# Image 0's fusion, tokens, mixtures and the weights' mixing moved under image 1's gathers

## The chip, the cores and the metric

The kernel runs on one core of a Trainium2 chip. The metric is the device time of one execution in microseconds (us); lower is better. The core has five engines with a queue each: TensorE (PE), VectorE (DVE), ScalarE (ACT), GpSimd (POOL) and SyncE (SP, which here only issues DMAs), and 16 DMA engines that they share.

## The reference

Two images of 128 channels and 64 x 64 pixels go through one layer, in float32:

```python
x = x + conv_ref(ln_c(x), ...)      # four deformable branches, pool branch, fusion
t = to_tokens(x)                    # (2, 4096, 128)
t = t + ffn_ref(ln_t(t), ...)       # spectral convolution + short mixtures
```

`conv_ref` has four deformable convolutions with 49, 1, 1 and 9 taps (60 in all) and 256 output channels each. For every tap and pixel an offset is computed, four neighbours are gathered, blended by bilinear weights and a mask, and contracted with that tap's 128 x 256 weights. Each branch is group-normalised and rectified, joined with a pooled branch, mixed by a 1 x 1 convolution to 128 channels (the fusion), group-normalised over the image and rectified again. `ffn_ref` normalises each token, convolves the sequence with 16 long filters (through a blocked Fourier transform), multiplies by matrices mixed from four sets with softmax weights, and adds a short three-step mixture (`M_u`).

## The kernel before

The program is a row of stages, each a block that all engines leave together.

`stage_normalise` prepares image 0: layer norm, a table of pixel rows in DRAM to gather from, and the first offsets. `stage_branches` is the long one. It works through 16 groups of 512 pixels (8 of image 0, then 8 of image 1) with 60 taps each, so 960 iterations n ("taps" below). Everything is written out by hand with semaphores; each engine runs its own `for n in range(...)` loop, in order:

- POOL: `gather(g, k, j)`, L509, four indirect DMAs of 128 rows for a tap, into one of RING = 6 buffers G. It waits until the tap six before has been blended (`blended`).
- ACT: `corner0` (L541), the first of the four corners times its weight into `ps_a`; `copy_out` (L549), transposed sum to `sT`.
- DVE: `blend` (L666 the other three corners times their weights, L670, L674, L677 the additions; L677 frees the buffer).
- PE: `turn` (L779, four transposes) and `contract` (L791, the tap's weights R times `sT`, accumulated in `ps_y`); and the offset convolution of the next groups (L761), spread over 52 of 56 taps.
- SP: loads and stores.

The offsets of later groups are computed beside this. The four pixel tiles of a group are handled two taps apart (`tile_at`: `rows` L618 to L633 and `weights` L639 to L646 on DVE, with L649 the end of a tile), at n = 100 + 56 i to 107 + 56 i. With k = n mod 60, at k = 54 DVE measures three branches' outputs (six L682), at k = 4 the last one. Image 1's layer norm runs in the same way under image 0's taps. R holds the weights of all 60 taps in SBUF for the whole stage.

Four stages follow for both images at once: `stage_fuse` (load y, rectify L1062, fuse L1024, copy L1042, statistics L1163; and beside it the weights' mixing: `mix` L1148 to L1153, rounding L1055, L1158, and the filters' transforms L1016, L1050, L1141), `stage_sum` (L1217, L1227), `stage_tokens` (16 chunks: L1345 to L1411, stores L1288 and L1294) and `stage_mixtures` (16 regions, L1460, L1449). Then `stage_spectral`, both images in one loop, and `stage_output`.

Of the kernel before, what the change touches and what calls it, by code (L numbers as in the profile page):

```python
# [3 lines left out]


B, C, H, W = 2, 128, 64, 64
HW = H * W
O = 256
# [27 lines left out]
NFC = 2 * (NBR + 1)  # L36
F32 = mybir.dt.float32
# [7 lines left out]
class Steps:  # L45
# [5 lines left out]
    def then(self, ins):  # L51
        self.n += 1
        ins.then_inc(self.sem, 1)
        self.eng.wait_ge(self.sem, self.base + self.n)

# [214 lines left out]

def stage_branches(nc, x, xn, tables, wom, R, ps_shared, base, P, rowt, regw, ident, eps6, om_dram, y_dram, ystats, xpart):

    ctx = ExitStack()
    with ctx:
        sb = lambda name, shape, dt=F32: ctx.enter_context(nc.sbuf_tensor(name, shape, dt))
        sem = lambda name: ctx.enter_context(nc.semaphore(name))
# [19 lines left out]
        yb = [sb(f"yb{h}", [128, 2, CH]) for h in range(3)]  # L296
        YB = (0, 1, 2, 1)
# [32 lines left out]
        r_loaded = pair("r_loaded")  # L330
        gathered = [sem(f"gathered{s}") for s in range(RING)]
# [25 lines left out]
        ln_step = sem("x1_step")  # L357

# [44 lines left out]
        def _(sp):  # L403
# [49 lines left out]

            sp.dma_start(R[:, 0:WIN_TAP, :], regw[:, 0:WIN_TAP, :]).then_inc(r_loaded[0], 16)
# [17 lines left out]
            for n in range(NT + 5):  # L472
# [25 lines left out]
                if c is not None:  # L498
                    store_xn(c)
            for h in range(3):  # L500
                sp.wait_ge(stored[h], 16 + 16 * YB.count(h) * NG)

# [25 lines left out]
        def _(act):  # L528
# [49 lines left out]

            for m in range(AHEAD):
                sigmoid(m)  # L580
            for n in range(NT + LAG + 1):
# [19 lines left out]
                if c is not None:  # L601
                    copy_x(c)

        @block.vector
        def _(dve):
# [102 lines left out]

            for m in range(AHEAD):
                rows(m)  # L710
                weights(m)
            spread(0)
            for n in range(NT + 5):
# [21 lines left out]
                if c is not None:  # L735
                    total_x(c)
            dve.wait_ge(measured, NBR * NG + 2)
# [3 lines left out]
        def _(pe):  # L741
# [40 lines left out]
            def contract(n):  # L782
# [4 lines left out]
                if k == t0:  # L787

                    pe.wait_ge(evacuated, g * NBR + br + 2)
                for half in range(2):  # L790
                    last = nc.tensor.matmul(ps_y[:, half, :], R[:, k, 128 * half:128 * half + 128],  # L791
# [11 lines left out]
            def turn_xn(c):  # L803
# [3 lines left out]
                last.then_inc(xn_turned, 1)  # L807

# [4 lines left out]
            for n in range(NT):  # L813
# [19 lines left out]
                if c is not None:  # L833
                    turn_xn(c)
            for n in range(NT - LAG, NT):
# [9 lines left out]
def group_affine(dve, act_sem, st, sq, var, sd, a, b, gm, gamma, beta, ready, nc):  # L845

    st.then(nc.vector.tensor_tensor(sq, gm[:, 0, :], gm[:, 0, :], ALU.mult))
    st.then(nc.vector.tensor_tensor(var, gm[:, 1, :], sq, ALU.subtract))
    st.then(nc.vector.tensor_scalar(var, var, 0.0, None, ALU.max))
    dve.sem_inc(ready, 1)  # L850
    dve.wait_ge(act_sem, 1)
    st.then(nc.vector.reciprocal(sd, sd))
    st.then(nc.vector.tensor_tensor(a, gamma, sd, ALU.mult))
    st.then(nc.vector.tensor_tensor(b, gm[:, 0, :], a, ALU.mult))
    st.then(nc.vector.tensor_tensor(b, beta, b, ALU.subtract))


def stage_fuse(nc, gate, y_dram, ystats, xpart, pool_w, fuse_w, gnp, gnf, blk16, blk8, eps5, fu, fa, fb,
               phi, dft_taps, m_phi, m_u, sigma, logw, gumbel, mus, mh, ml, hot, kern_dram):

    ctx = ExitStack()
    with ctx:
        sb = lambda name, shape, dt=F32: ctx.enter_context(nc.sbuf_tensor(name, shape, dt))
        sem = lambda name: ctx.enter_context(nc.semaphore(name))
        pw = sb("pw", [C, O])
        fw = sb("fw", [128, NFC, C])
        gp = sb("gp", [128, 2, B, NFC])
        gf = sb("gf", [C, 2, B])
        mv = sb("mv", [128, B, 2 * NBR, 2])
        me = sb("me", [128, 2, B * NFC])  # L870
        gm = sb("gm", [128, 2, B * NFC])
        sq = sb("sq", [128, B * NFC])
        var = sb("var", [128, B * NFC])
        sd = sb("sd", [128, B * NFC])
# [1004 lines left out]
```

## Time and profile before

| | us |
|---|---|
| median of 3 runs (6341.73 to 6343.83) | 6341.98 |
| the profiled execution | 6341.62 |
| its span, first to last instruction | 6339.8 |
| mean granted TensorE clock in it | 0.937 |

The profile is of one execution. The page has busy times by engine, the span in 40 slices, and the costliest groups of instructions; the trace behind it answers questions by line, by stretch of time, by wait and in order of time. All rows used are shown further down. In them "issue" as a releaser means that an engine waited for nothing that the profile shows, and "SPq" is SP's queue.

### The profile page before, as it was taken

Reading aid. Unit: us, or ns where it says so; the run is one execution under the profiler, and the core shown is the slowest. Engines: PE = TensorE matmul, PEld = TensorE weight load, DVE = VectorE, ACT = ScalarE, POOL = GpSimd, SP = SyncE. Lnnn points to the kernel's source line nnn. Section 1 sums busy time; section 2 is a strip of 40 time slices with the busy share of each in tenths; the row PEclk is TensorE's granted clock in tenths of the full one; section 3 lists DMA queues with packets and bytes.
Section 4 is the critical chain, followed back from the end, with each engine's and each line's share of the span. In section 5 each row is a group of like instructions: output and inputs, shape, how many; then the busy total and the mean of one; then the engine's idle time right before and its main releaser. Section 6 shows DMA issues by size and latency. Waiting matters only on the chain. (4 is left out here: it accounts for less than half of the span.)

```text
span 6339.8 us, 66182 instructions
## 1 busy us (share of the span) xinstructions
PE 5183.8 (82%) x16608; PEld 2621.9 (41%) x16608; DVE 4852.1 (77%) x6696; ACT 2639.3 (42%) x6416; POOL 3943.7 (62%) x4379
## 2 busy tenths in 40 slices
PE   6987878888887888888787878875666759999998
PEld 5333333333333333333233333322222337777777
DVE  5897888878887888878788887878777364666664
ACT  1343434333333434333333333433333633666663
POOL 4777777777777777777777777777777002222221
PEclk8999999999999999999999999998888979999999
DMA  7777777777777777777777777777777864555555
GB/s 242 219 239 222 238 227 229 227 220 230 216 226 218 224 223 222 220 226 217 227 215 233 210 232 209 230 209 230 216 215 219 308 220 135 149 146 151 152 149 178
DMA packets 565020, 1349.89 MB, mean 213 GB/s; under 512 B 95111, under 2 KB 244490, under 8 KB 563338
## 3 DMA queue, kind: packets, MB, share of 16 engines
q0 software_dynamic: 328480, 1045.08, 56.4%
q1 hardware_dynamic: 216922, 282.50, 13.9%
q10 hardware_dynamic: 19344, 19.20, 0.9%
q8 instruction: 106, 1.74, 0.1%
q14 instruction: 168, 1.38, 0.1%
HBM read 1240.28 MB, written 106.13 MB: 212 GB/s over the span
## 5 line engine op out<-in xcount | busy, mean ns | idle before, releaser
L509 POOL DMA_INDIRECT G<-table,om x3840 | 3660.3, 953 | 1199.0 <-issue 1160.3
L666 DVE TENSOR_TENSOR G<-G,ps_w 128x1536 f32<-128x1536 f32 x960 | 1681.5, 1752 | 491.5 <-DMA G<-table,om 475.2
L791 PE MATMUL ps_y<-sT,R 128*128 128x512 f32 x3840 | 2015.7, 652 | 25.7 <-ACT yb L557 25.7
L541 ACT ACTIVATE ps_a<-G,om 128x128 f32<-128x128 f32 x3840 | 1192.6, 357 | 1871.6 <-DMA G<-table,om 1196.7
L779 PE MATMUL ps_t<-ident,acc 128*128 128x128 f32 x3840 | 661.9, 298 | 948.3 <-DVE acc L677 928.8
L779 PEld LDWEIGHTS ps_t<-ident,acc 128*128 128x128 f32 x3840 | 433.3, 147 | 1698.7 <-DVE acc L677 1587.0
L549 ACT ACTIVATE sT<-ps_t 128x512 f32<-128x512 f32 x960 | 572.1, 596 | 1073.3 <-PE ps_y L791 1070.8
L791 PEld LDWEIGHTS ps_y<-sT,R 128*128 128x128 f32 x3840 | 721.1, 208 | 592.6 <-issue 590.0
L1587 DVE TENSOR_TENSOR vl<-ps_v,vh 128x512 fp32r<-128x512 f32 x1024 | 657.4, 686 | 335.3 <-ACT vh L1536 335.1
L1521 POOL DMA_DIRECT2D ut<-spec_dram x512 | 262.5, 513 | 853.4 <-PE ps_v L1602 638.8
L670 DVE TENSOR_TENSOR ps_a<-G,ps_a 128x512 f32<-128x512 f32 x960 | 668.5, 696 | 131.6 <-ACT ps_a L541 32.9
L677 DVE TENSOR_TENSOR acc<-G,ps_a 128x512 f32<-128x512 f32 x960 | 659.8, 687 | 103.0 <-DVE ps_a L674 4.1
L1536 ACT ACTIVATE vh<-ps_v 128x512 fp32r<-128x512 f32 x1024 | 580.3, 596 | 356.7 <-PE ps_v L1602 331.3
L761 PE MATMUL ps_c<-xr,wom 128*128 128x512 f32 x1470 | 719.6, 610 | 0.0
L761 PE MATMUL ps_shared<-xr,wom 128*52 128x512 f32 x1470 | 718.5, 609 | 0.0
L674 DVE TENSOR_TENSOR ps_a<-G,ps_a 128x512 f32<-128x512 f32 x960 | 667.0, 695 | 31.8
L761 PEld LDWEIGHTS ps_c<-xr,wom 128*128 128x128 f32 x1470 | 292.2, 200 | 381.1 <-issue 381.1
L1625 PE MATMUL ps_yf<-vh,mh 128*128 128x512 f32 x1024 | 413.6, 404 | 0.0
L1625 PE MATMUL ps_yf<-vh,ml 128*128 128x512 f32 x1024 | 411.2, 402 | 0.0
L1625 PE MATMUL ps_yf<-vl,mh 128*128 128x512 f32 x1024 | 409.2, 400 | 0.0
L1602 PE MATMUL ps_v<-tt,ut 96*128 96x512 f32 x1024 | 367.9, 401 | 15.6 <-DMA ut<-spec_dram 13.8
L761 PEld LDWEIGHTS ps_shared<-xr,wom 128*52 128x52 f32 x1470 | 154.6, 126 | 503.2 <-issue 503.2
(187 smaller groups left out, 2386.4 us busy)
## 6 DMA issues: line engine op xcount, KB each, us to landing
tt<-kern_dram SPq DMA_DIRECT2D x512, 192.0 KB, 3.3
G<-table,om POOLq DMA_INDIRECT x3840, 3.7
y_dram<-yb SPq DMA_DIRECT2D x64, 512.0 KB, 4.8
yin<-y_dram SPq DMA_DIRECT2D x16, 2048.0 KB, 12.9
ut<-spec_dram POOLq DMA_DIRECT2D x256, 96.0 KB, 3.3
spec_dram<-spec_hi SPq DMA_DIRECT2D x64, 256.0 KB, 2.6
ut<-spec_dram POOLq DMA_DIRECT2D x256, 48.0 KB, 3.0
om_dram<-om_next SPq DMA_DIRECT2D x60, 150.0 KB, 3.5
```

What stands on the lines that cost most here:

```text
L509: pool.indirect_dma_start(G[k % RING][:, j, :], None, tables[g // GI], bass.IndirectOffsetOnAxis(ap=om[g % 2][:, j, 0, k:k + 1].bitcast(I3 ...
L541: last = nc.scalar.activation(ps_a[:, j, :], G[k % RING][:, j, 0:C], ACT.Copy, scale=om[g % 2][:, j, 1, k:k + 1])
L666: nc.vector.tensor_tensor(three, three, ps_w[:, :, h:h + 1].to_broadcast([128, 12, C]) .rearrange("p (j c) d -> p j c d", j=4), ALU.mult). ...
L670: nc.vector.tensor_tensor(ps_a[:, :, :], corner(1), ps_a[:, :, :], ALU.add).then_inc(added, 1)
L674: nc.vector.tensor_tensor(ps_a[:, :, :], corner(2), ps_a[:, :, :], ALU.add).then_inc(added, 1)
L677: nc.vector.tensor_tensor(acc[n % 3][:, :, :], corner(3), ps_a[:, :, :], ALU.add).then_inc(blended, 1)
L761: last = nc.tensor.matmul(ps_c2 if rest else ps_c[:, :], cols[:, 128:128 + REST] if rest else cols[:, 0:128], rows, start=(tap == 0), stop ...
L779: last = nc.tensor.transpose(ps_t[:, 128 * j:128 * j + 128], acc[n % 3][:, j, :], ident[:, :])
L791: last = nc.tensor.matmul(ps_y[:, half, :], R[:, k, 128 * half:128 * half + 128], sT[n % 2][:, :], start=(k == t0), stop=(k == ends[br] - 1))
L1536: nc.scalar.activation(vh[c][:, n, :, :], spread(ps_v[n % BANKS]), ACT.Copy).then_inc(v_high, 1)
L1587: nc.vector.tensor_tensor(vl[c][:, n, :, :], spread(ps_v[n % BANKS]), vh[c][:, n, :, :].bitcast(F32), ALU.subtract).then_inc(v_low, 1)
L1625: last = nc.tensor.matmul(ps_y[q][:, :], m[:, c, k, :], v[c][:, :, k, :], start=(c == 0 and k == 0 and n == 0), stop=(c == 1 and k == KF - ...
```

## The change

After tap 480 (FIRST) all of R that image 0 needs has been used. The change turns R into an `arena` whose space is then carved up for image 0's later work, and brings the contraction weights of image 1 through a ring of three buffers RR of two taps each (`load_ring`, 256 KB every second tap, waited for by `contract`). Each engine's loop gets a `side(n)` at the end of its iteration, which runs one small piece of image 0's later stages at a tap written out by hand:

| taps | what |
|---|---|
| 484 to 497 | parameters, means and group statistics |
| 500 to 507 | the softmax weights and the `M_u` mixture; `mus` is then stored to DRAM |
| 494 to 637 | fusion of image 0: one load, one rectification and one matmul every second tap, a copy and statistics every 16 |
| 638 to 655 | sum, one piece of 512 pixels every second tap |
| 657 to 763 | tokens, 8 chunks of 12 taps, and the edge |
| 760 to 792 | mixtures, 8 regions of 4 taps |
| 790 to 819 | the filters' transforms, 8 of 3 taps |
| 819 to 889 | mixing of the spectral weights, 8 pieces of 8 taps; the result goes to DRAM |

The later stages then handle image 1 alone, and `stage_fuse` loads `mus`, `mh` and `ml` from DRAM through POOL's queue. All semaphores of `stage_branches` are cleared by SP behind it, one after the other, where six were before. Two small constants are loaded in the first block.

```diff
-            R = held.enter_context(nc.sbuf_tensor("R", [C, TAPS, O], F32))
+            arena = held.enter_context(nc.sbuf_tensor("arena", [128, ARENA], F32))
+            R = arena[:, :].rearrange("c (t o) -> c t o", t=TAPS)
+        FIRST = GI * TAPS
+        FS, SS, TT, TP, MM, MP, WK, KP, WM, WP = 500, 640, 660, 12, 760, 4, 793, 3, 822, 8
+            def load_ring(q):                                   # SP
+                if q >= RSLOTS:
+                    sp.wait_ge(summed, FIRST + RTAPS * (q - RSLOTS + 1))
+                k = RTAPS * q % TAPS
+                sp.dma_start(RR[q % RSLOTS][:], regw[:, k:k + RTAPS, :]).then_inc(rr_loaded[q % RSLOTS], 16)
...
+                q = every(n, FIRST - 2, RTAPS, GI * TAPS // RTAPS)
+                m = every(n, FS - 6, 2, 2 * NBR * GI)           # load_y(m)
+                k = every(n, SS - 2, 2, GI)                     # load_sum(k)
+                    c = every(n, TT + 9 + 4 * half, TP, NCH)    # store_spec(c, half)
+                j = every(n, WK + KP, KP, NK)                   # store_kernel(j)
+                c = every(n, WM + 2, WP, NM - 1)                # load_m(c + 1)
+                c = every(n, WM + SEG + 3, WP, NM)              # store_m(c)
...
+                m = every(n, FS - 1, 2, 2 * NBR * GI)           # ACT: relu_y(m)
+                g = every(n, FS + 4 * NBR, 4 * NBR, GI)         # copy_fused(g)
+                k = every(n, SS, 2, GI)                         # relu_fu(k)
+                c = every(n, TT + 3, TP, NCH)                   # root_t(c)
+                c = every(n, TT + 6, TP, NCH)                   # copy_uT(c)
+                    c = every(n, TT + 8 + 3 * half, TP, NCH)    # round_spec(c, half)
...
+                g = every(n, FS + 4 * NBR + 2, 4 * NBR, GI)     # DVE: statistics of fu
+                k = every(n, SS + 1, 2, GI)                     # add_x(k)
+                c = every(n, TT + 2, TP, NCH)                   # measure_t(c)
+                c = every(n, TT + 3, TP, NCH)                   # normalise_t(c)
+                    c = every(n, TT + 8 + 3 * half, TP, NCH)    # split_spec(c, half)
+                r = every(n, MM + 3, MP, NCH)                   # add_mixture(r)
+                j = every(n, WK + 2, KP, NK)                    # split_kernel(j)
+                    c = every(n, WM + i, WP, NM)                # mix(c, i), i = 0..3
+                if every(n, WM + SEG, WP, NM) is not None:      # combine()
+                c = every(n, WM + SEG + 2, WP, NM)              # split_mixed(c)
...
+                m = every(n, FS, 2, 2 * NBR * GI)               # PE: fuse(m)
+                c = every(n, TT, TP, NCH)                       # turn_t(c)
+                c = every(n, TT + 4, TP, NCH)                   # turn_u(c)
+                    c = every(n, TT + 6 + 3 * half, TP, NCH)    # transform(c, half)
+                    r = every(n, MM + late, MP, NCH)            # mix_region(r, late)
+                j = every(n, WK, KP, NK)                        # transform_kernel(j)
...
                 # contract(n), PE
+                if g < GI:
+                    taps = R[:, k, :]
+                else:
+                    q = (n - FIRST) // RTAPS
+                    if k % RTAPS == 0:
+                        pe.wait_ge(rr_loaded[q % RSLOTS], 16 * (q // RSLOTS) + 16)
+                    taps = RR[q % RSLOTS][:, k % RTAPS, :]
...
-                for s in [xn_turned, xn_copied, xn_summed, xn_stored, table_written, ln_step]:
+                for s in sems:
                     sp.sem_clear(s)
...
+        @block.gpsimd                                           # stage_fuse
+        def _(pool):
+            pool.dma_start(fw[:], fuse_w).then_inc(fw_loaded, 16)
+            pool.dma_start(flat(mus[:]), mus_dram).then_inc(mus_loaded, 16)
+            pool.wait_ge(z_ready, GI)
+            for i, t in ((0, mh), (1, ml)):
+                pool.dma_start(flat(t[:]).bitcast(F32), m_dram[i].rearrange("c s k e -> c (s k e)")).then_inc(m_loaded, 16)
```

`every(n, first, step, count)` gives the index of the piece that is due at tap n, or None. The comments that name pieces are this document's.

## Rows read from the trace of the kernel before

**Rows 1.** The page's costliest groups: the gathers and the first step of the blend.

```profile
L509 POOL DMA_INDIRECT G<-table,om x3840 | 3660.3, 953 | 1199.0 <-issue 1160.3
L666 DVE TENSOR_TENSOR G<-G,ps_w 128x1536 f32<-128x1536 f32 x960 | 1681.5, 1752 | 491.5 <-DMA G<-table,om 475.2
```

**Rows 2.** Who POOL waited for in 64:4938: us in total, times, longest us.

```profile
POOL G L509 <- DVE acc L677: 13.2, 29, 3.7
```

**Rows 3.** Windows: us, then PE, PEld, DVE, ACT, POOL busy (x), clock, DMA, GB/s.

```profile
2900.00:3100.00 200.00, 167.46 (x486) 66.86 (x484) 164.64 (x187) 78.66 (x214) 151.54 (x160) 1.00 0.75 221
3700.00:3900.00 200.00, 167.69 (x474) 71.67 (x474) 171.57 (x232) 74.18 (x206) 150.77 (x159) 0.94 0.74 217
4500.00:4700.00 200.00, 126.09 (x318) 55.06 (x316) 157.15 (x169) 76.89 (x208) 151.53 (x160) 0.81 0.75 220
```

**Rows 4.** Timeline of POOL: start us, us, engine, line; in brackets the idle before.

```profile
3763.01 0.95 POOL L509 DMA_INDIRECT G<-table,om  x1 [0.85 <-DVE acc L677]
```

**Rows 5.** Timeline of DVE: L677 of taps 716, 724, 729 and 733.

```profile
3706.86 0.69 DVE L677 TENSOR_TENSOR acc<-G,ps_a 128x512 f32<-128x512 f32 x1
...
3762.05 0.69 DVE L677 TENSOR_TENSOR acc<-G,ps_a 128x512 f32<-128x512 f32 x1
...
3783.30 0.69 DVE L677 TENSOR_TENSOR acc<-G,ps_a 128x512 f32<-128x512 f32 x1
...
3799.25 0.69 DVE L677 TENSOR_TENSOR acc<-G,ps_a 128x512 f32<-128x512 f32 x1
```

**Rows 6.** DMA queues and issues in 2600:4900: queue, packets, MB, share; us to landing.

```profile
q0 software_dynamic: 146179, 479.12, 71.1%
...
G<-table,om POOLq DMA_INDIRECT x1828, 3.7
```

**Rows 7.** Windows of the four stages behind the gathers, in order.

```profile
4938.68:5101.32 162.64, 124.28 (x284) 54.35 (x284) 60.20 (x136) 116.78 (x176) 0.00 (x0) 0.92 0.86 312
5101.32:5123.06 21.74, 0.00 (x0) 0.00 (x0) 16.69 (x16) 12.71 (x16) 0.00 (x0) 0.50 0.62 194
5123.06:5219.49 96.43, 52.29 (x200) 30.23 (x200) 64.34 (x242) 30.20 (x70) 0.11 (x1) 0.84 0.75 273
5219.49:5281.53 62.04, 56.43 (x384) 53.26 (x384) 11.00 (x16) 0.00 (x0) 0.00 (x0) 0.94 0.17 68
```

**Rows 8.** Timeline of ACT in the fusion: first rectifications, four copies.

```profile
4951.07 11.38 ACT L1062 ACTIVATE yin<-yin,ybb,ya 128x512 f32<-128x512 f32 x16 [4.11 <-DMA yin<-y_dram]
4965.65 0.69 ACT L1042 ACTIVATE fu<-ps_f,bias 128x512 f32<-128x512 f32 x1 [3.20 <-PE ps_f L1024]
...
5080.40 0.69 ACT L1042 ACTIVATE fu<-ps_f,bias 128x512 f32<-128x512 f32 x1 [1.01 <-PE ps_f L1024]
5087.27 0.69 ACT L1042 ACTIVATE fu<-ps_f,bias 128x512 f32<-128x512 f32 x1 [0.55 <-PE ps_f L1024]
...
5094.14 0.69 ACT L1042 ACTIVATE fu<-ps_f,bias 128x512 f32<-128x512 f32 x1 [0.71 <-PE ps_f L1024]
```

**Rows 9.** Timeline of SP: ends of the first two stages, first token store, edge stores.

```profile
53.50 0.60 SPq L157 DMA_DIRECT2D xn<-xnpad  x1
59.57 0.34 SPq L454 DMA_DIRECT2D R<-in_regw  x1
...
4934.82 0.36 SPq L432 DMA_DIRECT2D y_dram<-yb  x1
...
5138.69 1.24 SPq L1288 DMA_DIRECT2D spec_dram<-spec_hi  x2
...
5213.77 1.27 SPq L1294 DMA_DIRECT2D spec_dram<-edge_hi  x2
```

**Rows 10.** Groups by line: the weights' mixing (4600:5100), the sum (5103:5330).

```profile
L1150 DVE SCALAR_TENSOR_TENSOR mw<-mr,wi,mw 128x1024 f32<-128x1024 f32 x12 | 15.4, 1285 | 0.4
L1158 DVE SCALAR_TENSOR_TENSOR ml<-mt,sigma_b,mh 128x256 fp32r<-128x256 f32 x16 | 6.6, 477 | 0.0
...
L1227 DVE TENSOR_TENSOR accum<-t_rb,t_xg 128x512 f32<-128x512 f32 x16 | 16.7, 1096 | 5.0 <-DMA t_xg<-in_x 4.8
```

More of the change, by code:

```diff
@@ new lines, in stage_branches @@
+        mu = Carve(arena[:, UT_AT:MU_AT]).take(SEG, 3, C)
+        uT = Carve(arena[:, UT_AT:MU_AT]).take(2, S + 1, NB)
+        back = Carve(arena[:, MU_AT:ARENA])
+        mus = back.take(3, SEG, C)
+        un = back.take(4, C)
+        xg = [xw[:, :], back.take(CH)]
+        small = Carve(arena[:, MU_AT + back.at:ARENA])
+        kern = Carve(arena[:, UT_AT:MU_AT])
+        windows, taps_dft = kern.take(2, 2 * S * KF), kern.take(4, NF)
+        khi, klo = ([kern.take(2 * S * KF).bitcast(F32R) for h in range(2)] for i in range(2))
@@ new lines, in normalise_t, with split_spec @@
+            def normalise_t(c):
+                dve.wait_ge(tsd_ready, c + 1)
+                ts.then(nc.vector.reciprocal(t_rs, t_sd))
+                for j in range(4):
+                    last = nc.vector.tensor_scalar(un[:, j, :], ps_s[:, j, :], t_mv[:, j, 0:1], t_rs[:, j:j + 1],
+                                                   ALU.subtract, ALU.mult)
+                last.then_inc(u_ready, 1)
+            def split_spec(c, half):
+                dve.wait_ge(hi_ready, 2 * c + half + 1)
+                nc.vector.tensor_tensor(lo[:, half, :], side_ps, hi[:, half, :].bitcast(F32), ALU.subtract)\
+                    .then_inc(lo_ready, 1)
@@ new lines, in turn_u, with transform @@
+            def turn_u(c):
+                pe.wait_ge(u_ready, c + 1)
+                for j in range(4):
+                    last = nc.tensor.transpose(ps_s[:, j, :], un[:, j, :], ident[:, :])
+                last.then_inc(u_turned, 1)
+            def transform(c, half):
+                if half == 0:
+                    pe.wait_ge(uT_ready, c + 1)
+                    pe.wait_ge(dft_loaded, 32)
+                else:
+                    pe.wait_ge(lo_ready, 2 * c + 1)
+                nc.tensor.matmul(side_ps, fwd[:, half, :], flat(un), start=True, stop=True).then_inc(transformed, 1)
@@ new lines, in transform_edge, with mix_region @@
+            def transform_edge():
+                pe.wait_ge(lo_ready, 2 * NCH)
+                for half in range(2):
+                    last = nc.tensor.matmul(ps_s[:, half, :], fwd_edge[:, half, :], un[:, 3, :], start=True, stop=True)
+                last.then_inc(edge_done, 1)
+            def mix_region(r, late):
+                p, q = chunks[r]
+                if r == 0:
+                    pe.wait_ge(edge_zeroed, 1)
+                    pe.wait_ge(mus_ready, SEG)
+                    pe.wait_ge(elo_ready, 1)
+                elif not late:
+                    pe.wait_ge(m_added, r)
+                last = mix_tokens(nc, ps_s, mus, uT, p, q, SEGMENTS[SEG - 1:] if late else SEGMENTS[:SEG - 1])
+                if late:
+                    last.then_inc(mixed, 1)
@@ L1421, with mix_tokens, stage_mixtures @@
 SEGMENTS = ((0, 16, 0), (16, 32, 1), (32, 64, 2), (64, 128, 3))
-def stage_mixtures(nc, accum, uT, mus, t_dram):
+def mix_tokens(nc, out, mus, uT, p, q, segments):
+    for lo, hi, seg in segments:
+        for lag in range(3):
+            src, shift = (p - lag) % 2, (p - lag) // 2
+            s0 = 1 + 4 * q + shift
+            last = nc.tensor.matmul(out[:, :, lo:hi], mus[:, lag, seg, :], uT[:, src, s0:s0 + 4, lo:hi],
+                                    start=(lo == 0 and lag == 0), stop=(lag == 2), skip_group_check=True)
+    return last
+def stage_mixtures(nc, b, accum, uT, mus, mus_loaded, t_dram):
     ctx = ExitStack()
```

1062 lines of the change are left out of this document (701 added, 361 removed).

## The prediction

> **What bounds the kernel now.** I read the costliest groups of the page first, then the waits, the windows, and last the timeline around one burst. The groups give the pace of the long stage: 3840 gathers of 0.953 us with 1199.0 us idle between them, of which 1160.3 is "issue" [rows 1]. One gather takes 0.95 + 0.30 = 1.256 us, a tap of four 5.03 us, and 960 taps 4826 us of the 6339.8. POOL is the bound there: DVE waits 475.2 us for gathers to land [rows 1], while POOL waits for DVE's last addition only 29 times, 13.2 us in all [rows 2]. The windows say the same: 159 or 160 gathers in each 200 us, whether DVE is busy 157 or 172 us, and whether PE's clock is 1.00 or 0.81 [rows 3].
>
> Behind the gathers nothing hides anything: four stages of 162.64, 21.74, 96.43 and 62.04 us, 342.85 in all, with POOL idle [rows 7]. They handle two images. After the change they handle one, and the other's work must fit into the gather stage without costing POOL.
>
> **How much room there is.** A buffer is used again six taps later, after 6 x 5.03 = 30.2 us. It needs three more issues (3 x 1.256 = 3.8), a landing (3.7 [rows 6]) and a blend. The blend's pitch shows where DVE catches up: four blends in 3799.25 - 3783.30 = 15.95 us, 3.99 each [rows 5]. So in a quiet stretch a buffer is free 30.2 - 11.5 = 18.7 us before POOL wants it. That is the reserve, and DVE refills it by 5.03 - 3.99 = 1.04 us a tap.
>
> What empties it is in the code before already: the tile bursts. In the worst one eight blends take 3762.05 - 3706.86 = 55.2 us, where POOL's pace is 40.2, a drain of 15.0 [rows 5]; the three measures at k = 54 just ahead take the rest, and POOL then waits, 0.85 us instead of 0.30 [rows 4]. There are seven such bursts under image 1 (taps 492, 548, ..., 828). In the other bursts some 1 to 5 us must be left, since the 29 waits sum to 13.2 us, of which 29 x 0.30 is the usual gap [rows 2].
>
> **What the tail gives back.**
> - Fusion. It begins as before: first rectification 12.4 us into the stage (4951.07 - 4938.68), first copy at 27.0 (4965.65) [rows 8]. Behind that PE sets the pace when nothing else is mixed in: two copies 6.87 us apart [rows 8]. Seven more groups take 48.1, and what follows the last copy (statistics, group sums, root, affine) takes about 5.3, from the last copy at 5094.14 to 5101.32 [rows 7, 8], less four `split_mixed` of 0.48 that stood between [rows 10]. Sum 27.0 + 48.1 + 5.3 = 80.4 against 162.64: saves 82. The long pitch before came from the mixing and transforms beside it, (162.64 - 80.4) / 8 = 10.3 us a group; they go too.
> - Sum: 16 additions of 1.10 with little between [rows 10], 8 fewer: saves 9.
> - Tokens: the stores of 16 chunks and one edge take 5213.77 - 5138.69 = 75.1 [rows 9], 4.45 us a chunk after 3.9 for the edge's six stores. Saves 8 x 4.45 + 3.9 = 39.
> - Mixtures: 62.04 less some 9 us of start and last store is 53 for 16 regions, 3.3 each [rows 7]; saves 26.
>
> Together **157 us**. The reloads of `mus`, `mh` and `ml` (0.8 and 4.2 MB) cost nothing if the last rectification frees them in time: at the stage's rate of 312 GB/s [rows 7] 4.2 MB take 13.5 us, and PE's last group, its copy, the group statistics and the sum stage lie above them. Without that cover they would add up to 13 us.
>
> **What it costs.**
> - Two more constant loads in the first block: 1 us.
> - The clears. The branch stage gets about 125 semaphores where 6 were cleared. Bounds: the first stage clears 24 and has 59.57 - 53.50 = 6.1 us from its last issue to the next stage's first; the branch stage clears 6 and has 4938.68 - 4934.82 = 3.9 [rows 7, 9]. If all of 2.2 us is 18 clears, one costs 0.12 us and 119 cost 14; if it is the stores' landing, 0. I take 6, in the middle since both are mixed.
> - DVE. The moved work is half of the four stages' DVE time without the mixing, plus the mixing: (152 - 36) / 2 + 36 = 94, and with gaps and the two more copies per piece 100 to 120 us [rows 7, 10]. DVE's landing waits alone, 475.2 us over both images [rows 1], are more than that, so on average it fits. Not in the bursts. Walking through the tap numbers: burst 660 meets chunk 0 of the tokens (2.9 us) and, five to nine taps earlier, four `add_x` of 1.1; the prices are 64.34 / 16 = 4.0 us a chunk, of which two thirds are its measuring and normalising, 11.00 / 16 = 0.69 for an addition and half of L1150's 1.285 for a mixing step [rows 7, 10]; burst 716 meets `split_spec` twice, one `measure_t` and `normalise_t`, and the chunk before (6 us); 772 meets three additions (2.1); 828 meets the mixing, four steps of 0.65, two `split_mixed` of 0.48 and a `combine` put at 1.6, 5.2 in eight taps. With the reserves left, 716 overflows by 5.5, 772 by 1, 828 by 2.5: 9 us. The first three bursts get under 1 us each and hold.
> - Landing. Ring, y loads and stores add 131 KB a tap each to the gathers' 1.09 MB. Gathers fill 71.1% of the DMA engines [rows 6]; the ring, at the gathers' own price per byte, adds 8.5 points, a second stream as much again: 75 becomes 83 to 92%. They land later. That lowers the reserve at the start of a burst; I take 1.5 us at four bursts, 6 us (bounds 0 and 4 each).
> - PE. Under full clock it is busy 167 of 200 us [rows 3], 4.2 a tap. The mixtures add 3.3 every 4 taps, 0.83: 5.03, exactly POOL's pace, for taps 760 to 792, with a burst in them. It delays the refill, not the steady pace; in the 9 us above.
> - ACT: 78.66 of 200 us busy [rows 3] leaves 3 us a tap; at most a rectification of 0.8 and a table load fall in one. Nothing, unless in a burst.
> - SP's waits: each piece waits for something due a tap or more earlier, and a ring load is issued five taps (25 us) before `contract` needs it. Even behind two other transfers of 4 to 13 us it lands in time. POOL's queue gets nothing in this stage.
>
> Sum: 6341.6 (the profiled execution, 0.4 below the median) - 157 + 1 + 6 + 9 + 6 = **6206 us**, 2.1% faster.
>
> **A rule weighed.** DVE gets new operations with both inputs in SBUF: `add_x` 8 x 1.1, `split_mixed` 16 x 0.48, and three of the `M_u` mixture, some 18 us in all [rows 10]. If each held POOL for its length, they would all be lost, since POOL has no slack. The tile work has such operations too, and windows with it and without it both have 159 or 160 gathers [rows 3]; so I give it nothing in the sum and 18 in the range. The Trainium skill (SBUF — State Buffer, Who interferes with whom) says that a DVE instruction with two SBUF inputs contends only with a GpSimd instruction that reads SBUF, and that a 2-port mode locks GpSimd out fully; by the second sentence only copies, casts and `tensor_scalar` within SBUF would cost, a few us here. The trace agrees as far as small ones go.
>
> **Rivals.**
> - *The bursts overflow broadly* (chance 0.18): PE at its limit stops the refill, ACT's pieces come late, DVE's side work finds empty reserves in all seven bursts. Each burst then loses the side work of its refill, some 17 taps of 0.25 us on average plus its own, 6 us or more: 7 x 6 to 7 x 10 in place of 15, so 6233 to 6261. If all of DVE's moved work fell on POOL, 120 in place of 15: 6311. For it speaks the wait in [rows 4]; against it that only 29 waits exist.
> - *The gathers lose pace* (0.06), the case on the other side. If the added streams bring the DMA engines to their limit, landings back up and POOL waits everywhere in image 1. It decides from 157 - 22 = 135 us over 480 taps, 0.28 us a tap (5.03 becomes 5.31, 5.6%). For it: 75% becomes up to 92%. Against it: the fusion runs at 312 GB/s in the mean [rows 7], above the 275 that would be asked of it here. At 0.4 us a tap: 6206 + 192 = 6398. The Trainium skill (DMA: Bandwidth & Descriptors, Queues, rings and completion order) says an engine serves its queues in turn, a packet at a time, so a load would not just fill the gaps but delay gathers; by it this rival is possible as soon as the share nears 1.
> - *The tail does not shrink so* (0.04): the reload through POOL's queue is late, or the short fusion is bound by loads; 13 to 25 us back, 6219 to 6231.
> - *Less is lost than I say* (0.12): no overflow, no clears: 6341.6 - 157 + 1 = 6186, or a few less.
>
> The forecast's own case, 6195 to 6218, has 0.60. The range is 6181 to 6258: it takes in the third and fourth cases and most of the first. Within 0.2% is about what a measurement of this kernel can tell from no change. Only the second rival reaches it: faster 0.94, same 0.01, slower 0.05.
>
> **What would show it.** Four stages behind the gathers of about 81, 13, 57 and 36 us. Gathers in 2500 to 4940 at 159 or 160 per 200 us but for a few windows, with POOL's waits for the blend's last addition under 30 us in sum, most of them at bursts 716 to 828. Gather landing near 4.5 us at the median and a DMA share of 0.83 to 0.92. PE's clock above 0.9 to the end of the mixtures. I am wrong if POOL's waits lie in every burst or between them, if `contract` waits for the ring, or if the stretch between the last y store and the fusion is over 15 us.

## The result, and the profile after

The changed kernel takes 6203.16 us (median of 4 runs, 6199.41 to 6208.11), the kernel before beside it 6341.85 (6339.43 to 6343.83). The ratio is 0.9782, with an interval of 0.9765 to 0.9799. The forecast was 6206.

The profiled execution took 6199.41 us, the fastest of the four, with a span of 6197.6; the one of before took 6341.62. The 142.2 us between them are what the traces can account for. First the page's groups and POOL's waits over the whole branch stage, which answer to [rows 1, 2]:

```profile
L756 POOL DMA_INDIRECT G<-table,om x3840 | 3661.8, 954 | 1205.2 <-issue 1153.9
L1012 DVE TENSOR_TENSOR G<-G,ps_w 128x1536 f32<-128x1536 f32 x960 | 1680.5, 1750 | 377.4 <-DMA G<-table,om 358.9
```
```profile
POOL G L756 <- issue: 1153.9, 3786, 0.3
POOL G L756 <- DVE acc L1023: 25.9, 50, 4.6
POOL G L756 <- DVEq L995: 25.4, 4, 8.5
```

The gathers keep their 954 ns and the 0.30 us between them. DVE's waits for them to land fall from 475.2 to 358.9 us: that is where the moved work went. POOL's waits for the blend's last addition rise from 29 to 50 in number and from 13.2 to 25.9 us, of which 50 x 0.30 is the usual gap.

The windows that answer to [rows 3], and one of the weights' mixing (columns as there):

```profile
2900.00:3100.00 200.00, 186.16 (x534) 77.12 (x533) 164.81 (x190) 93.54 (x238) 151.53 (x160) 0.99 0.84 272
3700.00:3900.00 200.00, 170.89 (x504) 75.13 (x502) 179.92 (x276) 81.57 (x218) 149.98 (x159) 0.97 0.86 276
4300.00:4500.00 200.00, 116.68 (x318) 51.29 (x317) 187.15 (x251) 78.73 (x215) 148.05 (x155) 0.83 0.86 285
4500.00:4700.00 200.00, 123.41 (x332) 53.30 (x330) 169.57 (x192) 80.27 (x217) 151.64 (x159) 0.85 0.82 257
```

Only 4300 to 4500 stands out, with 155 gathers for 160. It holds the one long wait of image 1, POOL's timeline at tap 841 (the other long ones are at taps 1 to 6, in both kernels alike):

```profile
4322.58 0.95 POOL L756 DMA_INDIRECT G<-table,om  x1 [0.30 <-issue]
4328.11 0.95 POOL L756 DMA_INDIRECT G<-table,om  x1 [4.58 <-DVE acc L1023]
4329.37 0.95 POOL L756 DMA_INDIRECT G<-table,om  x1 [0.30 <-issue]
```

And what DVE did ahead of it: the last of the burst's tile rows (L976, L979), the six group statistics of the tap with k = 54, and the four operations of `combine`, before the blend of a tap begins at L1012:

```profile
4318.53 0.19 DVE L979 CAST om_next<-a 128x60 int32<-128x60 f32 x1
4318.76 3.66 DVE L1028 BATCH_NORM_STATS2 ystats<-yb 128x6 f32<-128x512 f32 x6
4322.33 0.41 DVE L1138 COPY arena<-ps_side 128x256 f32<-128x256 f32 x1
...
4323.45 0.41 DVE L1141 TENSOR_TENSOR arena<-ps_side,arena 128x256 f32<-128x256 f32 x1
4323.78 1.75 DVE L1012 TENSOR_TENSOR G<-G,ps_w 128x1536 f32<-128x1536 f32 x1
```

The queues in 2600 to 4900, for [rows 6]: the gathers' share falls by 5 points, though they move the same bytes in the same number of packets, and the hardware queue's rises by 14.5, so the sum rises by 9.5. The gathers land half a microsecond later.

```profile
q0 software_dynamic: 145720, 477.60, 66.1%
q1 hardware_dynamic: 81568, 139.59, 17.8%
...
RR<-in_regw SPq DMA_DIRECT2D x229, 256.0 KB, 4.3
G<-table,om POOLq DMA_INDIRECT x1822, 4.2
```

The four stages behind the gathers, for [rows 7], and ACT's timeline in the fusion, for [rows 8]:

```profile
4954.79:5036.20 81.41, 60.04 (x140) 27.56 (x140) 12.64 (x48) 52.54 (x75) 2.23 (x4) 0.86 0.77 277
5036.20:5048.29 12.09, 0.00 (x0) 0.00 (x0) 8.34 (x8) 6.19 (x8) 0.00 (x0) 0.50 0.55 174
5048.29:5105.08 56.79, 30.27 (x101) 16.65 (x101) 32.24 (x121) 15.22 (x35) 0.10 (x1) 0.74 0.63 234
5105.08:5139.68 34.60, 29.02 (x192) 27.30 (x192) 5.50 (x8) 0.00 (x0) 0.00 (x0) 0.89 0.15 61
```
```profile
4967.36 11.38 ACT L1672 ACTIVATE yin<-yin,f_small 128x512 f32<-128x512 f32 x16 [6.99 <-DMA yin<-y_dram]
4982.14 0.69 ACT L1665 ACTIVATE fu<-ps_f,f_small 128x512 f32<-128x512 f32 x1 [3.40 <-PE ps_f L1651]
4982.73 5.73 ACT L1672 ACTIVATE yin<-yin,f_small 128x512 f32<-128x512 f32 x8
4989.01 0.69 ACT L1665 ACTIVATE fu<-ps_f,f_small 128x512 f32<-128x512 f32 x1 [0.55 <-PE ps_f L1651]
...
5030.21 0.69 ACT L1665 ACTIVATE fu<-ps_f,f_small 128x512 f32<-128x512 f32 x1 [6.18 <-PE ps_f L1651]
```

The end of the branch stage, SP's timeline, for [rows 9]: 11.11 us from the last y store's issue to the fusion's first, where there were 3.86.

```profile
4943.68 0.36 SPq L561 DMA_DIRECT2D y_dram<-yb  x1
4954.79 0.35 SPq L1632 DMA_DIRECT2D pw<-in_pool_w  x1
```

The account between the two profiled executions:

| part | before | after | difference |
|---|---|---|---|
| first gather's start | 64.91 | 64.59 | -0.3 |
| first to last gather | 4854.25 | 4861.94 | +7.7 |
| last gather to last y store | 15.66 | 17.15 | +1.5 |
| last y store to the fusion's first issue | 3.86 | 11.11 | +7.25 |
| four stages | 342.85 | 184.89 | -158.0 |
| all behind them, and around the span | 1060.1 | 1059.7 | -0.4 |

Of the 7.7 us all is placed to within 0.2: POOL's idle beyond its usual 0.30 adds up to 0.6 us at tap 510, 1.9 at 730 (1.0 before) and 4.8 at 841 and 842, and gathers that themselves last longer than 0.95 us add 1.6 us over image 1.

### The profile page after: what moved, and what is told of

It reads as the page before. It is cut to its first block and busy times, and to the rows that moved or that the text cites. A ratio compares the mean times of both kernels' runs of the same rounds, so it can differ in the third digit from the quotient of the medians.

```text
span 6197.6 us, 67010 instructions
## 1 busy us (share of the span) xinstructions
PE 5173.2 (83%) x16620; PEld 2628.7 (42%) x16620; DVE 4854.9 (78%) x6768; ACT 2642.1 (43%) x6429; POOL 3947.3 (64%) x4383
## 5 line engine op out<-in xcount | busy, mean ns | idle before, releaser
L1012 DVE TENSOR_TENSOR G<-G,ps_w 128x1536 f32<-128x1536 f32 x960 | 1680.5, 1750 | 377.4 <-DMA G<-table,om 358.9
L1307 PE MATMUL ps_y<-sT,RR 128*128 128x512 f32 x1920 | 1033.2, 667 | 14.7 <-ACT yb L804 10.3
L1307 PE MATMUL ps_y<-sT,arena 128*128 128x512 f32 x1920 | 988.6, 641 | 7.4 <-ACT yb L804 7.4
L1307 PEld LDWEIGHTS ps_y<-sT,RR 128*128 128x128 f32 x1920 | 369.0, 213 | 303.8 <-issue 301.1
L1307 PEld LDWEIGHTS ps_y<-sT,arena 128*128 128x128 f32 x1920 | 353.6, 204 | 284.7 <-issue 284.7
```

The source lines that it names most:

```text
L1012: nc.vector.tensor_tensor(three, three, ps_w[:, :, h:h + 1].to_broadcast([128, 12, C]) .rearrange("p (j c) d -> p j c d", j=4), ALU.mult). ...
L1307: last = nc.tensor.matmul(ps_y[:, half, :], taps[:, 128 * half:128 * half + 128], sT[n % 2][:, :], start=(k == t0), stop=(k == ends[br] - 1))
```

## The experiments

**The changed kernel again**, on the chip of the next three, e1_after_again.

> The changed kernel as it is, for the chip on which e2, e3 and e11 run. About 6203 us, 0.978 of the kernel before. The traces so far show 7.4 us lost by the gathers in image 1 (three spots: the first mixing burst at taps 510 to 512, the group statistics at 730, the mixing with the burst of 828), 11.1 us instead of 3.9 from the last y store to the fusion's first issue, and four stages of 81.4, 12.1, 56.8 and 34.6 us behind.

Measured: 6204.85 us (6202.62 to 6208.66, 5 runs), the kernel before on this chip 6345.85, ratio 0.9781 (0.9767 to 0.9794). The waits stand where they stood: 4.27 us more than the usual pitch at tap 841, 1.45 at 730, 1.16 at 510. Two things vary between executions. The usual pitch of a gather is 1.2576 us in the traces of before and after and 1.2586 here (1.2604 in e6), in image 0 as in image 1, with no wait to show for it; over the gathers of image 0 alone that is 1.2 us here and 5.8 in e6. And the longer gathers near tap 650 (below) cost 1.4 us here and 0.8 in the first trace.

**The clears split over five engines**, e2_clear_split.

```diff
     @clearing.sync
     def _(sp):
-        for s in sems:
+        for s in sems[0::5]:
             sp.sem_clear(s)
+    @clearing.tensor
+    def _(pe):
+        for s in sems[1::5]:
+            pe.sem_clear(s)
...
```

> The 125 semaphore clears at the end of the branch stage go 25 to each of five engines. If each clear costs SP 0.061 us one after the other (7.25 us for 119 more), the stretch from the last y store to the fusion's first issue falls from 11.1 to about 5 us and the kernel gains 6: 6197. The rival: the stretch is the landing of the last stores (the others' stores are more now), and nothing moves, within 1 us of the unsplit kernel. A third: other engines clear more slowly than SP, gain 3 to 4 us. The rest of the trace stays.

Measured: 6200.07 us (6199.41 to 6200.63), 4.8 less than the unsplit kernel's median beside it. SP's timeline:

```profile
4947.85 0.36 SPq L561 DMA_DIRECT2D y_dram<-yb  x1
4954.60 0.35 SPq L1652 DMA_DIRECT2D pw<-in_pool_w  x1
```

The stretch is 6.75 us in place of 11.11: 4.4 us gone by dividing the clears alone, with the same stores in flight. So the clears set what was added, and not the stores' landing. The trace has the clears themselves. In the changed kernel SP's 125 stand one behind the other from 4946.93 to 4954.52, 0.061 us each. Here SP's 25 are done at 4952.51, where its price alone would lead to 5.0 us for the stretch, but PE's 25 take 0.120 each, from 4951.36 to 4954.28, and all engines leave the block together. The other three take 0.08 each. So PE costs the missing 1.7 us, and the third case of the expectation, engines that clear more slowly than SP, came true in part.

**Two pieces moved off a burst**, e3_shift.

```diff
-FS, SS, TT, TP, MM, MP, WK, KP, WM, WP = 500, 640, 660, 12, 760, 4, 793, 3, 822, 8
+FS, SS, TT, TP, MM, MP, WK, KP, WM, WP, SW = 500, 640, 660, 12, 760, 4, 793, 3, 846, 8, 520
...
-                if n == FS:
+                if n == SW:
                     segment_max()
-                if n == FS + 3:
+                if n == SW + 3:
                     segment_weights()
-                i = every(n, FS + 4, 1, SEG)
+                i = every(n, SW + 4, 1, SEG)
```

> The weights' mixing starts 24 taps later (846 instead of 822), behind the burst of tap 828, and the mixture weights' preparation with the M_u steps comes 20 taps later (520 instead of 500), off the refill of burst 492. If the loss of 7.4 us is side work that finds a buffer reserve just drained, the waits at 841 (4.8 us) and at 510 to 512 (1.5) go, 5 to 6 us in all: 6197, and the last gather starts about 4921 us. The rival, that the same DVE and SBUF work costs POOL the same wherever it lies, or that the mixing delays later taps instead: no gain, the waits only move. The mixing now ends about tap 910; if that is too late the fusion's first groups wait and the kernel is slower than 6203.

Measured: 6199.40 us (6194.91 to 6202.77), 5.5 less than e1 by the medians, the ranges just touching. POOL's waits in 2550 to 4940, first the changed kernel, then this one:

```profile
POOL G L756 <- DVE acc L1023: 16.4, 30, 4.6
```
```profile
POOL G L756 <- DVE acc L1023: 10.9, 27, 2.3
```

The waits at 841 and 510 are gone. The same operations, 20 and 24 taps later, cost next to nothing in waits. What is left is at tap 730, 2.6 us here. Beyond the usual gap the waits of image 1 are 2.7 us, for 7.6 in e1 and 7.3 in the first trace.

**Both**, e11_both.

> Both edits together: if they are independent, 6 + 5 to 6 us, about 6191, 0.976 of the kernel before. If the gather stage's end is set by something that neither edit touches, one of the two gives nothing and it stays at 6197 or above.

Measured: 6195.38 us (6190.45 to 6199.58), ratio 0.9764 (0.9751 to 0.9778), 9.5 us less than the changed kernel beside it. The two gains add up, 4.8 + 5.5 = 10.3 against 9.5. This is the fastest of the kernels; its POOL waits in 2550 to 4940 are 9.5 us, 24 times, longest 1.5.

**Five gather buffers in place of six**, in the changed kernel (e4_ring5) and in the kernel before (e5_before_ring5).

```diff
-RING = 6
+RING = 5
```

> The changed kernel with five buffers for the gathers in place of six. The reserve model: a buffer is wanted five taps later and not six, so every burst has 5.03 us less reserve, 13.7 in place of 18.7, and nothing changes between the bursts. Walking the blend's times of the changed kernel through it gives about 36 us more, 6239, in waits at the bursts of both images, deeper in image 1 (where 5 of 7 bursts had under 2 us left) than in image 0. The rival, that POOL is held by contention (port, DMA) and the buffers have nothing to do with it: no change, 6203. If DVE were at its average limit in image 1, waits would stand between the bursts too and the time would rise by over 80 us.

> The kernel before with five buffers. By the same model about 22 us more than before, 6364: each of the sixteen bursts drains 15 to 18 of a reserve of 13.7. Beside the changed kernel with five this shows how much of the reserve the moved work takes: the difference between the two should be 14 us smaller than with six buffers. Rival: no change, 6342.

Measured: 6246.78 us (ratio to before 0.9848, 0.9833 to 0.9863) and 6373.46 us (1.0050, 1.0034 to 1.0065). The changed kernel loses 0.0066 x 6342 = 42 us by it, the kernel before 31.5. POOL's waits in 2550 to 4900, the changed kernel with five and then the kernel before with five:

```profile
POOL G L756 <- issue: 548.7, 1799, 0.5
POOL G L756 <- DVE acc L1023: 48.6, 39, 8.1
```
```profile
POOL G L509 <- DVE acc L677: 18.5, 24, 3.6
```

So the buffers' reserve is what stands between DVE and POOL. Behind the first six taps every wait beyond the usual gap lies at the end of a burst or just behind it (in the changed kernel 2.5 us at 504, 1.8 at 560, 0.8 at 616, 2.8 at 672, 3.5 at 728, 2.7 at 784, 7.8 at 840, each with smaller ones beside it); between the bursts there is none. The expectations' model was 6 us low for the one and 9.5 for the other; 5 of them are the start, where POOL fills five buffers and stands before the first blends, which it left out. The difference between the kernels, 11 us, is near its 14. Beyond the usual gap POOL waits in image 1, with five buffers, 37 us with the moved work and 11.4 without it; with six, 7.3 and 1.0. The sixth buffer hides most of it.

**The ring alone in the kernel before**, e6_ring_only.

```diff
+            def load_ring(q):
+                if q >= RSLOTS:
+                    sp.wait_ge(summed, FIRST + RTAPS * (q - RSLOTS + 1))
+                k = RTAPS * q % TAPS
+                sp.dma_start(RR[q % RSLOTS][:], regw[:, k:k + RTAPS, :]).then_inc(rr_loaded[q % RSLOTS], 16)
...
-                    last = nc.tensor.matmul(ps_y[:, half, :], R[:, k, 128 * half:128 * half + 128],
+                    last = nc.tensor.matmul(ps_y[:, half, :], taps[:, 128 * half:128 * half + 128],
```

> The kernel before, with only the contraction weights' ring for image 1 (131 KB more a tap through SP's queue), nothing moved. If the gathers' pace is POOL's own, the time is that of before within 2 us, 6344, the DMA share rises by 4 to 9 points and the gathers' landing by 0.1 to 0.4 us. If the ring's traffic costs pace (the rival that ended slower), it is 0.05 us or more a tap, 24 us or more. If contract waits for the ring, DVE's waits for PE grow and it shows at the bursts only.

Measured: 6341.32 us against 6341.93, ratio 0.9998 (0.9989 to 1.0007), so the ring costs 4 us at most. The profiled execution is the slowest of the eleven, 6348.48 us; its wider pitch of 1.2604 us is the same in image 0, where no ring runs, so it isn't the ring's. The queues in 2600 to 4900:

```profile
q0 software_dynamic: 145923, 478.29, 67.3%
q1 hardware_dynamic: 52439, 85.17, 11.2%
...
G<-table,om POOLq DMA_INDIRECT x1825, 3.8
```

The hardware queue's share rises by 7.9 points with the ring (the forecast had 8.5), but the gathers' falls by 3.8 with the same bytes, so the DMA engines go from 0.75 to 0.79 only: shares of two queues don't add up. The gathers land after 3.8 us for 3.7. PE never waits for a ring load.

**More traffic still.** e7_extra_stream adds two loads of 131 KB a tap to the changed kernel, into a tile that is idle then; e12_copy_stream adds the same amount as copies within DRAM, over eight places.

```diff
+            def load_extra(e):
+                for h in range(2):
+                    if e:
+                        sp.wait_ge(rx_loaded[h], 16 * e)
+                    sp.dma_start(flat(xnp[:, 4 * h:4 * h + 4, :])[:, 0:O], regw[:, (2 * e + h) % TAPS, :]).then_inc(rx_loaded[h], 16)
```
```diff
+            def copy_extra(e):
+                if e >= 8:
+                    sp.wait_ge(rx_done[e % 8], 16 * (e // 8))
+                sp.dma_start(rx_dram[e % 8], regw[:, e % TAPS, :]).then_inc(rx_done[e % 8], 16)
```

> The changed kernel with two more loads of 131 KB a tap for taps 486 to 925 into a tile that nothing uses then (it computes the same). The DMA engines go from a share of 0.84 to about 1.0. If the DMA share is what the gathers' pace would have broken on, landings grow from 4.2 to well over 8 us and POOL waits between the bursts, 50 us or more in all. If only the landing matters for the reserve, each us of landing costs one us at each of seven bursts: landing 6 us, about 13 us more, 6216. If neither, 6203.

> The changed kernel with two copies of 131 KB a tap from DRAM to DRAM in taps 486 to 925, over eight places, so that SP does not wait for them (it computes the same). In the run with two more loads a tap SP stood 91 of 145 us around tap 830 waiting for these loads, issued the mixing's 1 MB load 33 us late, and DVE waited 14.7 and 5.7 us for loads; POOL lost 22.7 us at taps 836 to 842, against 4.8 without. If the loss came from SP being late and not from the landing of the gathers, it goes here: waits of 5 to 6 us at 841, and in the other bursts up to 2 us each for a landing of 4.8 us or more, 6205 to 6213. If it is the DMA engines' share itself, 6226 or more as there, with late landings between the bursts.

Measured: e7 6226.73 us (0.9819, 0.9804 to 0.9834), e12 6206.17 us (0.9786, 0.9769 to 0.9802). Both raise the DMA share in 2600 to 4300 from 0.85 to 0.94; only e7 is slower than the changed kernel, by 0.0037 x 6342 = 23 us. Its losses are not spread: of the 30.9 us that POOL idles in image 1 beyond the usual gap, 22.7 lie in taps 836 to 842. DVE's waits in 2550 to 4940 say why, and SP's waits in 4200 to 4345 say what is behind them:

```profile
DVE ps_side L1144 <- DMA arena<-in_m_phi: 14.7, 1, 14.7
DVE om_next L991 <- DMA om_dram<-om_next: 11.5, 4, 5.7
```
```profile
SPq L594 <- DMA xnp<-in_regw: 90.8, 38, 7.0
```

SP issues in order and waits for each extra load's predecessor, which was issued only a tap earlier. It stood 90.8 of 145 us in these waits and fell behind: the mixing's 1 MB load went out at 4253.4 where the changed kernel's went at 4220.6, 33 us late with gathers that were 6 us late, and DVE, in order too, stood before a mixing step with the blends of all taps queued behind it. Its four waits for `om_dram` are for stores, which SP issues as well; they lie at taps 554, 723, 778 and 837, all in bursts, and the changed kernel has none of them. POOL lost 4.0 us more than there at 728 to 730 and 1.8 at 561. In e12, where SP waits for none of its copies, DVE has no such wait, and POOL's waits in 2550 to 4940 are 20.3 us for 16.4. So 18% more bytes (729.77 MB for 618.56, in 2600 to 4900) cost the gathers about 4 us of waits, which the times can't tell from nothing (the intervals of e12 and the changed kernel overlap), and loads issued late cost 22.7 - 4.8 = 18 at one place. That e12's copies don't write SBUF, as e7's loads do, is a difference that was not tried by itself.

**What makes a gather longer.** In the changed kernel five gathers of image 1 last 1.14 to 1.34 us and a sixth 1.10; before, none of that length is there, the longest of taps 301 to 899 has 1.04. Each of them starts inside a DVE operation with two SBUF inputs (`add_x`, the `M_u` mixture, `split_mixed`). Three kernels put one more DVE operation of 128x512 into every second tap from 301 to 899 of the kernel before; only the operation differs. Its result isn't used.

```diff
+                if 300 <= n < 900 and n % 2:
+                    if n > 301:
+                        dve.wait_ge(extra, (n - 301) // 2)
+                    nc.vector.tensor_tensor(flat(xnp[:])[:, 0:CH], xw[:, :], flat(xnp[:])[:, 0:CH], ALU.add).then_inc(extra, 1)
```

In e9_one_sbuf the second input is `flat(ps_s[:, :, :])`, in PSUM; e10_copy has `nc.vector.tensor_copy(flat(xnp[:])[:, 0:CH], xw[:, :])`.

> The kernel before with one more DVE addition of 128x512 in every second tap of 301 to 899 (300 in all, about 0.6 us each, into a tile that is overwritten later; the result is the same), both inputs in SBUF. In the changed kernel every gather longer than 1.1 us starts inside a DVE operation with two SBUF inputs. If such an operation holds a gather that starts in it, some 100 or more of the 2400 gathers of this stretch become 1.15 to 1.75 us long instead of 0.954, at most 0.6 us for each operation: 30 to 120 us more. If the long gathers of the changed kernel had another cause (its added transfers), none appear here, and only a few us are lost in the bursts, to 6350. This and the next two differ only in the operation.

> The same with the second input in PSUM. If the cause is two SBUF inputs at once, the gathers keep 0.954 us, and what is lost is the reserve at the bursts alone: 6342 plus 2 to 8 us. If any DVE work that reads and writes SBUF holds a gather, it is as slow as the one with two SBUF inputs.

> The same with a copy from SBUF to SBUF, about 0.3 us long. If a copy locks POOL out while it runs, gathers that start inside it are up to 0.3 us longer, some 50 of them, 5 to 15 us in all; if not, 6342 plus 0 to 4 us.

| kernel | us | ratio (interval) | the 300 operations | gathers of 1.11 us and more | gathers' excess over 0.953 |
|---|---|---|---|---|---|
| before | 6341.91 | | | 0 | 0.9 us |
| e8, two SBUF inputs | 6369.56 | 1.0040 (1.0026 to 1.0055) | 206.8 us | 61 | 25.3 us |
| e9, SBUF and PSUM | 6344.83 | 1.0004 (0.9994 to 1.0014) | 204.7 us | 0 | 1.1 us |
| e10, copy in SBUF | 6358.08 | 1.0025 (1.0014 to 1.0036) | 128.8 us | 44 | 13.7 us |

The excess (summed over the gathers of taps 301 to 899 that last over 1.0 us) is most of the difference in time (27.7 us for e8, 16.2 for e10). One operation and one gather of each kernel, DVE's and POOL's timelines; e8:

```profile
1674.96 0.69 DVE L741 TENSOR_TENSOR xnp<-xw,xnp 128x512 f32<-128x512 f32 x1
```
```profile
1675.10 1.38 POOL L510 DMA_INDIRECT G<-table,om  x1 [0.30 <-issue]
```

e9:

```profile
1754.11 0.69 DVE L741 TENSOR_TENSOR xnp<-xw,ps_side 128x512 f32<-128x512 f32 x1
```
```profile
1754.26 0.95 POOL L510 DMA_INDIRECT G<-table,om  x1 [0.30 <-issue]
```

e10:

```profile
1739.48 0.43 DVE L741 COPY xnp<-xw 128x512 f32<-128x512 f32 x1
```
```profile
1739.63 1.11 POOL L510 DMA_INDIRECT G<-table,om  x1 [0.30 <-issue]
```

In e8 the operation ends at 1675.65 and the gather at 1676.48, 0.83 us later; in e10 the ends are 1739.91 and 1740.74, 0.83 again. A gather that starts inside such an operation ends 0.82 to 0.83 us after the operation does, if its own 0.95 us are not over later still: its last 0.83 us have to wait for the operation's end, its first 0.12 don't. In e9, 136 gathers start inside the added operation and none is held. The expectation for e8 began at 30 us: it is 27.7. In its trace 88 gathers start inside one of the 300 operations, where the expectation counted on 100 or more.

The other order is not the mirror of it. In e8, 237 of the additions start while a gather is already running, and they take 0.68 to 0.72 us, as long as in e9: a running gather doesn't hold them. The copy of e10 does meet one: 43 copies that start 0.42 to 0.51 us into a gather make it up to 1.05 us long (some 2 of the 13.7 us), and the eight that start 0.54 to 0.65 us into one take 0.55 to 0.66 us in place of 0.42.

## Why the prediction was right

**The tail, -157: measured -158.0.** The fusion 80.4 against 81.4, the sum 13 against 12.1, the tokens 57 against 56.8, the mixtures 36 against 34.6. Inside the fusion the first rectification starts 12.6 us in (12.4), the first copy at 27.35 (27.0), the last at 75.4 (27.0 + 48.1), all from the rows above. "PE sets the pace" holds too. From the end of the first copy to the start of the last PE is busy 47.34 of 47.38 us, a matmul every 0.429 us and 16 of them to a group, 6.87; ACT idles 0.55 us before each copy, for PE:

```profile
4982.83:5030.21 47.38, 47.34 (x111) 20.66 (x109) 4.86 (x7) 37.91 (x55) 1.06 (x2) 1.00 0.65 224
```

The 1.0 us that the fusion is over its forecast are 0.35 before the first copy and 0.7 behind the last (6.0 for 5.3). The reloads through POOL's queue cost nothing that shows.

**The constants, +1: nothing.** The gathers start 0.3 us earlier.

**The clears, +6: 7.25,** at 0.061 us each, in the middle of the bounds of 0 and 14. The forecast left open whether clears or stores set the stretch, and took the middle for that reason alone, so that it came near is luck; e2 settles it for the clears.

**Burst overflow +9 and later landing +6.** Together 15; measured 7.7 + 1.5 = 9.2 us, and not where it was put. The mechanism holds: e4 and e5 show that the reserve is what the side work is paid from and that all waits lie at bursts, e3 that the same work costs next to nothing some 20 taps on. e9 says it most plainly: 205 us of added DVE time for 2.9 us (interval -4 to 9). A burst drains about 15 us and the 48 taps behind it could refill 48 x 1.04 = 50, so side work between bursts is free; only what lies in a burst or just ahead of its end counts.

The reserve can be read from the traces: a tap's first gather starts so long after the end of the blend that freed its buffer. Between the bursts it reaches some 18.7 us in both kernels, as forecast. The lowest of each burst, where 0.3 means that POOL waited or just didn't:

| burst (tap) | 492 | 548 | 604 | 660 | 716 | 772 | 828 |
|---|---|---|---|---|---|---|---|
| before | 5.5 | 4.9 | 2.6 | 4.2 | 0.3 | 1.1 | 3.7 |
| after | 0.3 | 4.0 | 2.6 | 1.9 | 0.3 | 0.3 | 0.3 |

Six sizes were off:
- "716 overflows by 5.5": the added operations of taps 716 to 730 sum to 5.6 us, close to the 6 that the forecast counted. But the thirteen blends take 78.7 us for 76.4 before, 2.3 more, because DVE was not solid in a burst: its waits for PE's tile matmuls (2.8 us) shrink to 0.6. POOL lost 0.9 us more than before. The chunk ahead of the burst cost it little: the reserve at the burst's start is 17.4 us for 18.6.
- "The first three bursts hold": burst 492 did not. The softmax and the `M_u` steps add 7.2 us in its 14 taps, whose blends end 8.6 us later, and POOL lost 1.0 us at 510 to 512, 1.5 in e1. The forecast listed no side work for this burst, though some two dozen operations of 0.16 us and more stand in a row there.
- "828 by 2.5": 4.8. The eight taps end 5.3 us later than before, as forecast, but the reserve is lowest 13 taps in, where `combine` meets the six group statistics (3.66 us), and 9.6 us of side work lie in those taps.
- "772 by 1": nothing. The reserve fell from 1.1 to 0.3 us there, and POOL did not wait.
- "1.5 us at four bursts" for landing: it rose by 0.5 us, not 1.5, and e12 adds another 18% of bytes for 4 us.
- "75 becomes 83 to 92%": 0.84 in 2600 to 4900. The forecast added the new streams' shares to the gathers', which shrank as they came (e6), and put a tap's gathers at 1.09 MB, where 479.12 MB in 2300 us [rows 6] are 1.05.

So 5.8 us too much there, 1.0 in the stages, 1.3 in the constants and 0.4 behind them, against 1.25 too little for the clears: 7.2 us in all, which lead from the unrounded 6206.6 to the profiled 6199.4. That the median, 6203.16, is closer still is luck: the profiled execution is the fastest of the four, and its gathers have the narrower pitch (1.2576 us for 1.2586 in e1).

**The rule weighed.** The sum had nothing for DVE's two-input operations and the range 18 us. The runs show both wrong in kind: it does cost, but only where a gather starts inside the operation, and only the rest of it. In the changed kernel that is 1.7 us in the profiled execution and 2 to 5 in others (e12 has 4.0 us between taps 636 and 660 alone), for 18 us of such operations. The Trainium skill (SBUF — State Buffer, Who interferes with whom) says that the shared port pair is an exclusive lock which the loser waits for in full, that a DVE instruction with two SBUF inputs contends with a GpSimd instruction reading SBUF, and that one with at most one SBUF input outside the 2-port modes doesn't. By that rule e10 holds gathers and e9 doesn't; e8 does if a gather counts as an instruction that reads SBUF, which the Trainium skill doesn't say there: it tells of a probe in which a `tensor_tensor` did not stall a DMA. The trace decides for e8 (61, 44 and 0 gathers of 1.11 us and more in e8, e10 and e9). It does not agree with a lock that the loser waits for in full: the gather's first 0.12 us pass, and 237 additions that start in a running gather are not held. The forecast had read the rule as excluding the gathers, which was the error.

**The rivals.** The bursts did not overflow broadly: POOL's waits in image 1 are 16.4 us over 30 waits, 7.3 beyond the usual gap, and three of seven bursts hold all of them. The gathers did not lose pace: 159 or 160 in each window but one, and the usual pitch is 1.2576 us at a DMA share of 0.75 (before), 1.2575 at 0.84 (after) and 1.2575 and 1.2577 at 0.93 (e7, e12), so it is excluded up to there. What e7 found in its place is a rival that nobody had named: a queue that issues in order falls behind, and one late load stops DVE. In the bursts less was lost than forecast, but the whole did not come down to 6186.

**Signs named ahead.** The four stages, the place of the long wait and the landing (4.2 for 4.5) came as said. PE's clock did not: above 0.9 was forecast to the end of the mixtures, and the fusion had 0.86, the tokens 0.74, the mixtures 0.89 (0.92, 0.84 and 0.94 before, [rows 7]). It changed no stage by more than a microsecond or two against the forecast.

## What to carry to other kernels

Where one engine sets a steady pace and another follows through a ring of buffers, don't ask whether the follower has time on average; find the tap at which its reserve is lowest and add up what is placed in the dozen taps ahead of it. Work beside it is nearly free: here 205 us of it cost 2.9, and some 20 taps of delay took 5 us out of the kernel. Keep waits for landings out of an in-order queue that also issues what others need, and under a stream of indirect DMAs give DVE operations one operand in PSUM; a copy within SBUF costs too.

## What the hardware showed

- A gather that starts inside a DVE operation with two SBUF inputs, or a copy within SBUF, ends some 0.83 us after the operation does, whether 0.6 or 0.2 us of it were left; if less than 0.12 us are left it keeps its 0.95. Per added operation that is 25.3 / 300 = 0.08 us for a 0.69 us addition and 13.7 / 300 = 0.05 for a 0.43 us copy; with an operand in PSUM it is nothing. A gather that starts in the first 0.03 us of the addition is not held, and the addition takes 0.73 to 0.76 us for 0.69 (seven cases in e8). An addition that starts in a running gather isn't held (237 cases, 0.68 to 0.72 us).
- The gathers' issue pace doesn't feel the DMA engines' load: 0.95 + 0.30 us, a pitch of 1.258, at 0.75, 0.84 and 0.93 of share. Their landing moves from 3.7 to 4.2 and, in e7, 4.8 us. A second queue's share comes partly out of the first's: 7.9 points more for the ring, 3.8 less for the gathers.
- Clearing a semaphore costs SP 0.061 us, one behind the other; 125 of them at a stage's end are 7.6 us on the critical path. In e2 one costs 0.08 us on DVE, ACT and POOL and 0.12 on PE.
